# Four chains interleaved with attention: shares of a slot replaced by tables of places, and one iteration less of lag

## What is computed

```
x = attention(ln(x), ln(x), Wq1, Wkv1, Wo1, bo1) + x     # self-attention, 16 heads of 16
x = attention(ln(x), ctx,   Wq2, Wkv2, Wo2, bo2) + x     # cross-attention on the context
x = geglu_ff(ln(x), Wff1, bff1, Wff2, bff2) + x          # 256 -> 2 x 1024 -> 256
q, k, v = x @ Wq.T + bq, ctx @ Wk.T + bk, ctx @ Wv.T + bv
out = softmax(q @ k.T) @ v + x                           # one head of 256
```

## Time and profile before

| what | us |
|---|---|
| runs before, median of two (2012.71 to 2016.59) | 2014.65 |
| the profiled execution, its own time | 2012.95 |
| span of its first to last instruction | 2011.1 |
| start of attention (first L1452) to its end | 173.4 to 1811.3 |
| an iteration with all five stages, no new batch | 110.3 to 110.5 |
| mean granted TensorE clock | 0.924 of full |

### The profile page before, as it was taken

One profiled execution on the slowest core, in us unless ns is written; L12 is line 12 of the kernel. 1 busy time (PEld: TensorE's weight loads), 2 busy tenths in 40 slices (PEclk: granted clock), 3 DMA queues, 4 the chain that ended last, 5 costly groups with the idle time before them and its releaser, 6 DMA issues.

```text
span 2011.1 us, 33881 instructions
## 1 busy us (share of the span) xinstructions
PE 1730.8 (86%) x12897; PEld 1030.1 (51%) x12897; DVE 1109.6 (55%) x2207; ACT 980.1 (49%) x2034; POOL 272.5 (14%) x366
## 2 busy tenths in 40 slices
PE   4838998989898989898898989898898989897666
PEld 3522444455564646464555646454555555455455
DVE  1317776665747475654657575655656574714222
ACT  2313665555454545554554545454555545463132
POOL 3330121120211111110201111100000010101100
PEclk8767999999899999999999999999999999997687
DMA  5630132426314141436322141436140313122310
GB/s 165 138 121 28 53 80 67 96 61 104 87 50 80 45 87 46 89 78 108 80 52 68 48 87 43 83 74 112 27 89 23 75 39 59 52 50 51 65 33 6
DMA packets 188879, 140.86 MB, mean 70 GB/s; under 512 B 41987, under 2 KB 179117, under 8 KB 188461
## 3 DMA queue, kind: packets, MB, share of 16 engines
q1 hardware_dynamic: 188717, 138.70, 31.2%
HBM read 90.40 MB, written 47.71 MB: 69 GB/s over the span
## 4 chain that ended last, share of the span: by engine, by line
PE 63%; DVE 19%; DMA 5%; ACT 4%; issue 4%; SPq 3%; POOL 1%; ACTq 0%; POOLq 0%; DVEq 0%
PE ps_last L1383 9%; DVE mxh L1154 9%; PE ps_o L1464 9%; PE ps_max L1439 9%; PE ps_last L1392 6%; PE ps_s L1452 6%; PE ps_pre L1253 5%; DVE mx L1079 3%; PE ps_cross L1355 3%; PE ps_pre L1261 3%; DMA v<-v_s 2%; PE ps_cross L1343 2%; PE ps_last L1261 2%; PE ps_last L1245 1%; ACT probs L910 1%
## 5 line engine op out<-in xcount | busy, mean ns | idle before, releaser
L1154 DVE TENSOR_REDUCE mxh<-ps_max 128x1 f32<-128x512 f32 x1024 | 670.3, 684 | 397.8 <-PE ps_max L1439 396.0
L964 ACT ACTIVATE probs<-ps_s 128x512 f32<-128x512 f32 x1024 | 556.0, 598 | 382.7 <-PE ps_s L1452 379.4
L1439 PE MATMUL ps_max<-kst,qst 96*128 96x512 bf16 x1024 | 394.2, 400 | 55.9 <-DVE mxh L1154 47.6
L1464 PE MATMUL ps_o<-probs,vg 128*17 128x256 f32 x4096 | 333.1, 398 | 6.5 <-ACT probs L964 5.7
L1452 PE MATMUL ps_s<-qst,kst 98*128 98x256 bf16 x2048 | 326.8, 282 | 1.0 <-ACT probs L964 0.3
L1452 PEld LDWEIGHTS ps_s<-qst,kst 98*128 98x128 bf16 x2048 | 202.1, 100 | 93.5 <-issue 15.1
L1439 PEld LDWEIGHTS ps_max<-kst,qst 96*128 96x128 bf16 x1024 | 99.3, 99 | 209.3 <-DVE mxh L1154 156.0
L910 ACT ACTIVATE probs<-ps_cross 77x512 f32<-77x512 f32 x224 | 133.5, 596 | 76.4 <-PE ps_cross L1343 76.3
L1383 PE MATMUL ps_last<-y_hi,wff_hi 128*128 128x256 f32 x464 | 144.6, 312 | 21.9 <-DVE hT L1113 13.2
L1464 PEld LDWEIGHTS ps_o<-probs,vg 128*17 128x17 f32 x4096 | 70.1, 96 | 152.0 <-issue 115.0
L936 ACT ACTIVATE th<-ps_last,b_tanh 128x256 f32<-128x256 f32 x116 | 55.0, 474 | 172.3 <-PE ps_last L1383 172.0
(11 more groups left out here) (200 smaller groups left out, 1998.4 us busy)
## 6 DMA issues: line engine op xcount, KB each, us to landing
parts_s<-qk_parts SPq DMA_DIRECT2D x32, 384.0 KB, 3.1
o_s<-o_sb SPq DMA_DIRECT2D x64, 128.0 KB, 2.1
oT<-o_s SPq DMA_DIRECT2D x64, 128.0 KB
den<-o_s SPq DMA_DIRECT2D x64, 128.0 KB
o_s<-o_sb SPq DMA_DIRECT2D x32, 256.0 KB, 2.2
kst<-parts_s SPq DMA_DIRECT2D x16, 384.0 KB, 5.2
kst<-parts_s SPq DMA_DIRECT2D x48, 128.0 KB, 5.9
qst<-parts_s SPq DMA_DIRECT2D x64, 96.0 KB, 2.4
```

Source lines behind the costliest of these rows:

```text
L964: nc.scalar.activation(probs[:, step % 2, 2 * pair:2 * pair + 2, :].rearrange("p j q -> p (j q)"), ps_s[pair][:, :], ACT.Exp, scale=SCALE) ...
L1154: nc.vector.tensor_reduce(mxh[:, i // 2, i % 2:i % 2 + 1], ps_max[i % 2][:, :], AX_X, ALU.max).then_inc(g_mx, 1)
L1439: mm(ps_max[i % 2][:, :], qst[0:ROWS, h, q * P:(q + 1) * P], kst[0:ROWS, h, k * 512:(k + 1) * 512], start=True, stop=True).then_inc(g_mt, 1)
L1464: last = mm(ps_o[j * W:j * W + VW, 0:CH], vg[:, g, kt, j * VW:(j + 1) * VW], probs[:, step % 2, j, :], start=(kt == 0), stop=(kt == KT - 1 ...
```

## The change

The lags of `cross` and `last` become 6 and 7: `mid` and `cross` of a chunk run in one iteration, and there are 23 iterations (and one numbered -1, for steps placed ahead). In place of the common steps each chain has a table of places for each engine (`PRE`, `MID`, `CROSS`, `LAST`); a place may lie in the iteration before or after. The maxima of a unit take places 1 to 21, the pair reduction 22; the transposition and negation stand at place 0 of the next unit and the store of the shift at place 5. `pre` takes the bank `ps_cross`, the cross scores take `ps_pre` (freed from sharing with the values), the first five cross maxima stay on `ps_cross`, and FF1 alternates between `ps_last` and `ps_pre`. The keys and values of the context, and `m3`, `m3_b`, `vp`, are loaded for the first chunk of a batch only. The semaphore of the stored parts is split in one for q and one for k. The instructions that compute are otherwise the same. The core of the diff:

```diff
-MAX_LAG, ATT_LAG, MID_LAG, CROSS_LAG, LAST_LAG = 4, 5, 6, 7, 8
+MAX_LAG, ATT_LAG, MID_LAG, CROSS_LAG, LAST_LAG = 4, 5, 6, 6, 7
 NIT = NCH + LAST_LAG
-PRE_STEPS, MID_STEPS, CROSS_STEPS, LAST_STEPS = 8, 9, 36, 26
-
-PRE_AT, CROSS_AT, LAST_AT = (1, 5, 22), (0, 0, 24), (1, 1, 32)
...
-CROSS_LOAD, DEN_LOAD, DEN_INV, LAST_LOAD = 26, 25, 27, 29
+
 SUB = 3
-PV_PLACE, LAST_PLACE = 1, 1
+PLACES = SUB * SLOTS
+def at(slot, place=0):
...
+    return SUB * slot + place
+PRE = dict(
+    SP=(at(1, 2), at(6), at(8, 2)),
+    DVE=(at(-3, 1), at(-2, 1)),
+    POOL=(at(-3, 2), at(4), at(6, 1)),
+    PE=(at(0, 2), at(2, 2), at(4, 2), at(6, 2)),
+    ACT=(at(1, 1), at(3, 1), at(5, 1), at(7, 1)))
+MID = dict(
+    SP=(at(12) - PLACES, at(0, 1), at(2), at(2, 1), at(11)),
+    DVE=(at(2, 1), at(4, 1), at(5, 2), at(6, 2)),
+    POOL=(at(15) - PLACES, at(6, 1), at(9, 1)),
+    PE=(at(5), at(7, 1), at(8, 1)),
+    ACT=(at(8), at(9)))
+FF1_AT, FF2_AT, CROSS_AT = at(10), at(19, 1), at(23)
+MAX_AT = (at(13, 2), at(14, 2), at(15, 2), at(16, 2), at(17, 2)) + tuple(at(18, 1) + i for i in range(7))
+SCORE_AT = tuple(CROSS_AT + 3 * i // 2 for i in range(H))
+LAST = dict(
+    SP=(at(28) - PLACES, at(0, 2), at(2), at(2, 1), at(29)),
+    DVE=(at(2, 2), at(5), at(7), at(7, 2), at(9, 1)) + tuple(FF1_AT + SUB * m + 4 for m in range(FM)) + (
+        FF2_AT + 10, FF2_AT + 15, FF2_AT + 21, FF2_AT + 26),
+    POOL=(at(0, 2), at(7, 1), at(9)),
+    PE=(at(6), at(8)) + tuple(FF1_AT + SUB * m for m in range(FM)) + tuple(FF2_AT + i * 5 // 2 for i in range(4)) + (
+        FF2_AT + 11, FF2_AT + 14, FF2_AT + 20, FF2_AT + 23),
+    ACT=(at(8, 2),) + tuple(FF1_AT + SUB * m + 3 for m in range(FM)) + (FF2_AT + 12, FF2_AT + 18, FF2_AT + 21))
+CROSS = dict(
+    SP=(at(11, 1), at(21, 2), SCORE_AT[7] + 6, PLACES),
+    DVE=MAX_AT + (at(21),),
+    POOL=(),
+    PE=MAX_AT + (at(20, 2),) + tuple(
+        x for h in range(H) for x in (SCORE_AT[h],) + (SCORE_AT[h] + 2,) * (h % G == G - 1)),
+    ACT=tuple(x for h in range(H) for x in (SCORE_AT[h] + 1,) + (SCORE_AT[h] + 3,) * (h % G == G - 1)))
+PV_PLACE = 1
...
-MAX_LAST, MAX_PAIRED, MAX_TURN = 18, 19, 21
-O_STORE, UNIT_LOAD = 0, 2
+MAX_TURN, MAX_FIRST, MAX_LAST, MAX_PAIRED = 0, 1, 21, 22
+SHIFT_STORE, UNIT_LOAD = 5, 2
...
+def alone(n):
...
+    return n >= NCH + ATT_LAG
...
-        cross_max_banks = ([ps_cross, ps_pre], ps_s)
-        cross_banks = ([ps_cross, ps_cross], ps_s)
-        last_banks = ([ps_last, ps_last], [ps_last, ps_max[0]])
+        def max_bank(f, spare):
+
+            if spare:
+                return ps_s[f % 2]
+            return ps_cross if f < 5 or f % 2 == 0 else ps_pre
+
+        def max_before(f, spare):
+
+            return next((e for e in reversed(range(f)) if max_bank(e, spare) is max_bank(f, spare)), -1) + 1
+
+        def score_bank(h, spare):
+            return ps_s[h % 2] if spare else ps_pre
+
+        ff1_banks = [ps_last, ps_pre]
...
+        def walk(engine, n, chains, pre, mid, cross, last, att_work, max_work, tail, loads=lambda slot: None):
+
+            def advance(name, places, make, lag, now):
+
+                for first in (n - 1, n, n + 1):
+                    for _ in range(places[engine].count(now - PLACES * (first - n))):
+                        index = first - lag
+                        if 0 <= index < NCH:
+                            if (name, index) not in chains:
+                                chains[name, index] = make(index)
+                            next(chains[name, index])
 
             for slot in range(SLOTS):
                 for place in range(SUB):
-                    if has_max:
-                        max_work(SUB * slot + place)
-                    if has_att:
-                        att_work(slot, place)
-                    if place == LAST_PLACE and not late_last:
-                        advance(0, slot)
-                    if place == SUB - 1:
-                        advance(2, slot)
-                        if late_last:
-                            advance(0, slot)
-                        loads(slot)
-                    advance(1, slot, place, SUB)
+                    now = at(slot, place)
+                    max_work(now)
+                    att_work(slot, place)
+                    advance("pre", PRE, pre, 0, now)
+                    advance("mid", MID, mid, MID_LAG, now)
+                    advance("last", LAST, last, LAST_LAG, now)
+                    advance("cross", CROSS, cross, CROSS_LAG, now)
+                loads(slot)
...
-            def mid(o, has_pre):
-                sp.wait_ge(c_q2, o)
+            def mid(o):
                 sp.wait_ge(c_x[0], o)
                 sp.dma_start(x0[:, :, :], t["x"].rearrange("b s d -> (b s) d").rearrange(
                     "(c i p) d -> c p i d", i=TT, p=P)[o]).then_inc(c_x0, 16)
+                yield
                 for i in range(2):
                     sp.wait_ge(g_ost[i], (o + 1) * HG // 2 * 16)
                 rows = o1_s.rearrange("(o r) s -> o r s", o=NCH)[o]
                 load_den(0, rows)
-                load_sums(oT, rows, c_in)
                 yield
                 sp.wait_ge(c_rd[0], o + 1)
                 store_inv(0, rows)
                 yield
+                load_sums(oT, rows, c_in)
                 sp.wait_ge(c_inv[0], (o + 1) * 16)
                 load_inv(den, rows, c_in)
...
+                if o % CPB == 0:
+                    sp.dma_start(k2[0:3 * DH, :, :], k2_s.rearrange("(e x) b n -> b x e n", e=H // KD)[b]
+                                 ).then_inc(c_kv, 16)
+                    for i in range(3):
+                        rows = slice((3 + i) * DH, (4 + i) * DH)
+                        sp.dma_start(k2[rows, :, :], k2_s.rearrange(
+                            "(e d t) b n -> b t d e n", e=H // KD, t=3)[b, STACK[1][i]]).then_inc(c_kv, 16)
+                    sp.wait_ge(c_av, o * 4)
...
+                if o % CPB == 0:
+                    b = o // CPB
+                    sp.wait_ge(c_av3, o)
+                    sp.dma_start(m3_b[:, :], m_s[D:D + 1, :].rearrange("a (b n) -> b a n", b=B)[b]).then_inc(c_m, 16)
+                    sp.dma_start(m3[:, :, :], m_s[0:D, :].rearrange("(k p) (b n) -> b p k n", p=P, b=B)[b]).then_inc(c_m, 16)
+                    sp.dma_start(vp[:, :, :], vp_s.rearrange("(b a p) n -> b p a n", b=B, p=CT)[b]).then_inc(c_m, 16)
...
+                def max_work(now):
+                    unit, place = max_unit(n, now)
+                    if place == MAX_TURN and 0 < unit <= NU:
+                        dve.wait_ge(g_mT, unit)
+                        dve.wait_ge(g_shl, (unit - 1) * 32)
+                        negative(ps_max[0][0:PAIRS, 0:P], sh_hi, sh_lo, g_shi, g_slo, unit)
...
+                pe.wait_ge(a_vc, p)
+                pe.wait_ge(c_o, max(0, p - CROSS_LAG) * 4)
+                pe.wait_ge(a_xn, (p + 1) * 2)
+                turn(ps_cross, pre_x).then_inc(a_T, 1)
...
+            def cross(o):
+                spare = alone(o + CROSS_LAG)
+                pe.wait_ge(s_fflo, KD * FF1_PIECES)
+                for f in range(2 * Q2F):
+                    if f == 0:
+                        pe.wait_ge(c_q2stack, (o + 1) * 64)
+                        pe.wait_ge(c_kv, (o // CPB + 1) * 80)
+                        pe.wait_ge(a_vc, min(NCH, o + CROSS_LAG + 1))
+                        pe.wait_ge(c_o, o * 4)
+                    elif max_before(f, spare):
+                        pe.wait_ge(c_mx, o * 2 * Q2F + max_before(f, spare))
+                    elif not spare:
+                        pe.wait_ge(c_h, o * FM)
...
+                    if m == 1:
+                        pe.wait_ge(c_q2f, min(NCH, o + LAST_LAG - MID_LAG + 1))
+                    elif m > 1:
+                        pe.wait_ge(c_h, o * FM + m - 1)
...
+                def max_work(now):
+                    unit, place = max_unit(n, now)
+                    if place == MAX_TURN and 0 < unit <= NU:
+                        pe.wait_ge(g_mp, unit)
+                        nc.tensor.transpose(ps_max[0][0:PAIRS, 0:P], mxq[:, :], ident[:, :]).then_inc(g_mT, 1)
```

796 lines of the change are left out of this document (321 added, 475 removed).

## The result

After the change the kernel takes 2141.3 us (two runs, 2135.9 and 2146.7) for 2014.65 before. The ratio is 1.063, interval 1.051 to 1.075: slower, and the forecast of 1960 (1865 to 2045) was wrong. The profiled execution after has a span of 2134.1 us for 2011.1.

A forecast was written before the change was run, and what follows sets the result against it. TensorE (92 us own work, 18.5 waits of 110.5 an iteration) bounds it. Start 170, n = 5 and 6 64.9 and 87, full iterations 958, without `pre` 408, n = 20 94, batches 30, tail 148: 1960 us (1865 to 2045).

The forecast's parts named there:

- 1.5 us on the path: Slots 0 to 9: denominators take 13.5 us until mid's, 16 until last's; VectorE's standing still costs TensorE 1.5 us.
- 1.7 us (0 to 6): Slots 10 to 17: q2's store and load take 15 us, TensorE arrives after 13.5, so it waits 1.7.
- The old waits go: Plateau iteration: waits of slots 0 to 7 (8 us) and FF1 (5) go, new ones of 9.5 come; 106.5 for 110.4.
- Four without `pre` at 102: Plateau: four iterations without `pre` take 102 us each, 408 together, after 105.9 against 110.4 before.
- Slots 10 to 17, FF1: With two banks FF1's waits fall from 5 us to 1.5; own work 24.6, the stretch 28.6 with q2's wait.
- Slots 18 to 22: Sixth cross maximum waits 2.0 us for FF1's last product on `ps_pre`; transposition 0.8; the stretch takes 18.5 us.
- Set-up, "3 us less": Before attention: GpSimd's reciprocal deviation of chunk 4 moves ahead of the set-up, saving 3 us (between 0 and 8).
- Batches: Changes of batch: 5.6 us three times again, plus 4.6 each for context loads behind q2's load; together 30 us.
- Tail: Iterations n = 21 and 22: 92 and 56 us, so 148 for 199.8, bounds 135 and 175.
- The rule of the skill: DMA fit of about 2.0 us plus bytes at 436 GB/s puts q2's 768 KB at some 3.8 us; not used.
- The slower rival: Round trips rule: denominators 5 us and q2 6 to 7 on the path, iteration 115, total 2079; chance 0.12.
- three signs of being wrong: An iteration under 103 or over 112 us, VectorE's L1042 waiting over 4 us for DMA, a tail over 175.

The follow-up runs named there:

- run without the way: Kernel after, denominators of mid and last not inverted (no packed load, reciprocal, store; raw sums broadcast), output not the reference's: 2055.2 us.
- run with the queries of the chunk before: Kernel after, with cross loading the previous chunk's queries, so no store and load of the same queries in one iteration; output not the reference's: 2082.0 us.
- run without both ways: Kernel after, with raw sums broadcast instead of inverted denominators and cross taking the previous chunk's queries; output not the reference's: 1994.9 us.

## Why the prediction was wrong, step by step

- **Denominators, "1.5 us on the path".** The step that failed: how long the way of the denominators takes, and so what of it TensorE has to wait out. In iteration 11 the products came at 15.1 and 18.3 us where I had 13.5 and 16. TensorE was done with what stands ahead of `Wo1` after 12.8 us, so the 1.6 that `mid`'s product came late, and 0.8 by which it was longer than elsewhere (1.45 us for 0.69), fell on the path in full: a wait of 3.9. `Wo1`'s eight instructions then took 3.17 us and not 1.9, in a stretch of 9 us with a granted clock of 0.81. By the run without the way it costs 5.7 us in a full iteration. A reading is wrong behind the term, too: in the earlier trace rows the product waits for the load of `vp`, so that row doesn't time the broadcast; here the product starts 6.25 us after the broadcast's issue (819.25 to 825.50), for the 5.3 I took.
- **q2's way, "1.7 us (0 to 6)".** In iteration 11 the wait is 1.8, but that is luck. From the end of the last q2 group to the first cross maximum pass 16.6 us where I had 15, and TensorE comes 14.8 us after that group where I had 13.5; the two errors cancel. And 1.7 is not the ordinary case: the wait is 1.2 to 2.3 us in n = 7, 9, 11, 13 and 15, but 5.0 and 4.9 in n = 10 and 14, with a new batch for `cross`, and 3.7 and 4.6 in n = 8 and 12, where the key stacks of attention's next batch are loaded right ahead of q2's store, which then takes 5.0 and 5.7 us for 2.4 until the load behind it is issued. The mean over the full iterations is 3.2, and the run with the queries of the chunk before gains 3.0. The 4.6 more that I had for a new batch is 3.2.
- **What these two are of the error.** In n = 8 to 20 the iterations take 1520 us where I had 1384, batches included. The run without both ways takes 116 us less there; my sum had 42 for the two, and 14 of its batches. So some 60 of the 136 us are the two ways, and the rest is own work and waits that stand without them.
- **"The old waits go": 110.4 to 106.5.** This is the other half, and the runs without the ways show it. My sum without its 1.5 and 1.7 is 103.3; iteration 11 without both ways takes 109.4, with 31.8, 26.3, 20.6 and 30.7 us in the four stretches where I had 29.5, 26.9, 18.5 and 28.4. I had put 92 us of own work and 18.5 of waits into an iteration of before, and 13 of the waits were to go. But TensorE was busy 100.97 of 110.50 us there, so no more than 9.5 could be idle; without the ways it is still idle 8.1. The distances of starts, read in two slots and two groups, gave an own work that the whole iteration doesn't reach. The tables of places are worth 1.4 us an iteration, not 7.
- **"Four without `pre` at 102".** They take 117.8 on the mean. I took `pre`'s 4.5 us off, as the earlier trace rows have it. But `pre` was the cover of a way that stays as long: its work went, and the wait grew by 2.7 at `Wo1` (3.9 in iteration 11, 6.6 in 17). With both ways off, these iterations take 106.9 to 108.9.
- **Slots 10 to 17, FF1.** 28.3 for 28.6, but by two errors that cancel: there is no wait of TensorE for `hT` in them where I had 1.5, and TensorE is busy 26.24 us where I had 24.6 of own work.
- **Slots 18 to 22.** The wait for FF1's last product is 2.0, to the digit, but the stretch takes 21.6 for 18.5: slot 19 alone takes 2.7 more than in iteration 10, at a lower clock (below).
- **Slots 23 to 31.** 30.7 for 28.4. The waits of the cross scores are 2.2 for 3.1; I had left out the transposition of `x2` (0.9), and TensorE is busy 27.55 us where I had 25.3.
- **Slots 0 to 9 without the way.** 31.8 with the way gone for 29.5: last's transposition waits 1.9 for L1001, which has GpSimd's deviation in its chain. Not foreseen.
- **Set-up, "3 us less".** 7.8 more. GpSimd's piece did move, and with it VectorE's normalisation of chunk 4, which now stands ahead of the 13.7 us `memset` of `kst`. TensorE waits 13.0 us behind that for L985. I had counted one engine's instruction of the moved step and not the others'.
- **Batches.** 5.6 three times were taken as fixed. The kernel before with a batch's tables once has none of them left (its full iterations take 110.3 to 110.9). After, the key stacks ahead of q2's store still show: n = 8, 12 and 16 take 119.2, 120.3 and 119.7 us, n = 9, 11 and 17 take 116.3, 118.0 and 115.5.
- **Tail.** 159.7, within 135 to 175; iteration 6 at 94.6 for 87, with 11.4 us before its first use of `q2st`, where nothing covers q2's way.
- **The rule of the skill.** The Trainium skill, "DMA: Bandwidth & Descriptors", section on the anatomy of one DMA, gives the fit that the prediction quotes for transfers that GpSimd issues. The loads here are issued by SP, so the comparison did not test it. The sum made no use of it.

The slower rival is the nearest to what happened, and had 0.12: its mechanism is this one and its 5 us for the denominators are the 5.7 measured, but its 6 to 7 for q2 are too much (3.0), and its 115 an iteration and 2079 us too little, because it stood on the same own work. Of the three signs of being wrong, two came: full iterations over 112 (up to 120.3), and L1020 waiting 4.96 us for a DMA. The third, a tail over 175, did not.

## What to carry over

The denominators' way through DRAM took about as long whatever stood beside it, 14 to 16 us from the start of the iteration. Before two dependent stages are put into one iteration, lay the way's length beside what TensorE has in its order until then, and do it for the leanest iteration, not for the full one. In an order written out by hand a wait belongs to the whole engine: a VectorE that waits for a DMA, or a GpSimd step one position too early, stops the tiles of everybody, so room must be given where the data is first touched, and a place is only as good as what shares it. And try the dull part of a change alone: loading a batch's tables once is worth 37 us to the kernel before, and the rest of the change lost four times that. And before an iteration's waits are counted as a gain, hold them against the engine's idle time in the profile: here it was 9.5 us, and the sum had 18.5.

## What the hardware showed that I had not expected

**The same work at two levels.** Slot 19 of iteration 10 and of iteration 11 hold the same 34 matmuls. The first takes 4.1 us at a granted clock of 1.00 (2.4 GHz), the second 6.8 at 0.59, most of it at the lower level of 1.2 GHz:

```profile
764.90:769.00 4.10, 4.10 (x34) 2.85 (x32) 2.74 (x6) 1.08 (x2) 0.00 (x0) 1.00 0.00 0
880.20:887.00 6.80, 6.80 (x34) 4.26 (x33) 2.79 (x5) 1.09 (x2) 0.00 (x0) 0.59 0.00 0
```

In both TensorE had just stood 2.0 us for `hT`. The fall did not come in each iteration after the same wait, so the price of a wait of 2 us was 2.0 or 4.7. What decides between the two, no run here shows.

**VectorE beside GpSimd.** The product with the inverse denominators has two inputs in SBUF. It takes 0.69 us where GpSimd stands still, and GpSimd's 128x512 subtraction (L759) of `pre`'s split takes 1.15 us. In iterations 9 to 12 the subtraction begins 0.03 to 0.38 us earlier, and the product takes 1.32 to 1.67 us. In iterations 13 to 15 the product begins 0.14 to 0.23 us earlier: it takes its 0.69, and the subtraction 1.47 to 1.56. Iteration 10, then iteration 13, GpSimd and VectorE:

```profile
704.94 1.15 POOL L759 TENSOR_TENSOR qk_f<-qk_f,qk_parts 128x512 f32<-128x512 f32 x1 [2.03 <-ACT qk_f L871]
704.97 1.67 DVE L1020 TENSOR_TENSOR oT<-oT,den 128x512 f32<-128x512 f32 x1 [4.74 <-DMA den<-o_s]
```

```profile
1063.54 1.56 POOL L759 TENSOR_TENSOR qk_f<-qk_f,qk_parts 128x512 f32<-128x512 f32 x1 [2.03 <-ACT qk_f L871]
1063.40 0.69 DVE L1020 TENSOR_TENSOR oT<-oT,den 128x512 f32<-128x512 f32 x1 [4.57 <-DMA den<-o_s]
```

In all seven, the one that begins second ends 0.14 or 0.15 us before the end of the first plus its own length alone (706.64 for 706.10 + 0.69; 1065.10 for 1064.09 + 1.15). So they run one after the other, and the profile shows the waiting as a longer instruction and not as idle time. The Trainium skill, "SBUF — State Buffer", section on the two separate sides, says that a VectorE instruction with two SBUF inputs and a GpSimd instruction that reads SBUF lock each other out: the one that starts first has the ports for its whole instruction, and the other blocks. These numbers agree with that.
